# Whole products for the first pairs of layer 2 in a compressed interaction tower

## What is computed

```python
e = jnp.stack([tbl_0[ids[:, 0]], ..., tbl_31[ids[:, 31]]], axis=1)   # 1024 x 32 x 16
x0 = e
xk = x0
for W in (W0, W1, W2):                                             # 32 x 32 x 64, 32 x 64 x 64, 32 x 64 x 64
    xk = jax.nn.relu(jnp.einsum('bmd,bhd,mhk->bkd', x0, xk, W))
    outs.append(jnp.sum(xk, axis=2))
z = jnp.concatenate(outs, axis=1)                                  # 1024 x 192
h = jnp.concatenate([z, dense_ctx], axis=1)                        # 1024 x 208
h = jnp.maximum(h @ W_top1 + b_top1, 0.0)
h = jnp.maximum(h @ W_top2 + b_top2, 0.0)
y = h @ W_top3
```

## Time and profile before

| what | value |
|---|---|
| median of 3 runs | 631.96 us (630.64 to 633.41) |
| the profiled execution | 630.55 us |
| its span in the trace | 628.7 us |
| TensorE busy | 594.6 us, 95% |
| VectorE busy | 585.8 us, 93% |
| GpSimd busy | 443.2 us, 70% |
| ScalarE busy | 355.5 us, 57% |
| mean granted TensorE clock | 0.984 |

### The profile page before, as it was taken

One profiled execution on the slowest core, in us unless ns is written; L12 is line 12 of the kernel. 1 busy time (PEld: TensorE's weight loads), 2 busy tenths in 40 slices (PEclk: granted clock), 3 DMA queues, 4 the chain that ended last, 5 costly groups with the idle time before them and its releaser, 6 DMA issues.

```text
span 628.7 us, 8924 instructions
## 1 busy us (share of the span) xinstructions
PE 594.6 (95%) x3046; PEld 243.0 (39%) x3046; DVE 585.8 (93%) x398; ACT 355.5 (57%) x665; POOL 443.2 (70%) x305
## 2 busy tenths in 40 slices
PE   4398998999999999999999999999999999999988
PEld 4252332234343354334443354334443354334434
DVE  4759999999999989999999999999999999999873
ACT  0173754729394663829385574829385674829361
POOL 5767887888888884988878887988878460806120
PEclk9579999999999999999999999999999999999999
DMA  6899989994997689695999779795999789690000
GB/s 176 192 236 271 210 249 210 274 211 113 252 264 183 137 248 214 205 218 128 238 218 246 154 231 213 230 217 129 221 216 258 155 247 217 212 213 17 2 0 1
DMA packets 60175, 119.82 MB, mean 191 GB/s; under 512 B 15271, under 2 KB 33734, under 8 KB 60054
## 3 DMA queue, kind: packets, MB, share of 16 engines
q1 hardware_dynamic: 49414, 114.69, 73.7%
q0 software_dynamic: 7584, 1.96, 3.8%
q10 hardware_dynamic: 3152, 2.86, 1.7%
HBM read 115.27 MB, written 5.25 MB: 192 GB/s over the span
## 4 chain that ended last, share of the span: by engine, by line
PE 53%; POOL 21%; DVE 12%; issue 7%; ACT 3%; SPq 2%; DMA 1%; DVEq 0%; ACTq 0%; POOLq 0%
PE acc L968 47%; POOL emb L447 12%; POOL z_pool L472 8%; DVE z_dve L529 8%; PE psm L1071 2%; SPq L426 2%; PE psm L1079 2%; DMA x_rot<-in_tbl_dram 1%; DVE z_dve L549 1%; DVE x0b L698 1%; PE acc L983 1%; ACT xq L717 1%; ACT xq L725 1%; ACT xq L771 1%; PE psm L1086 1%
## 5 line engine op out<-in xcount | busy, mean ns | idle before, releaser
L529 DVE TENSOR_TENSOR z_dve<-xq,x0b 128x2048 f32<-128x2048 f32 x179 | 398.5, 2279 | 12.4 <-ACT xq L717 7.5
L968 PE MATMUL acc<-z_dve,w_cin 128*64 128x512 f32 x1688 | 387.2, 597 | 9.9 <-DVE z_dve L529 7.1
L472 POOL TENSOR_TENSOR z_pool<-x0b,xs 128x2048 f32<-128x2048 f32 x45 | 205.3, 4565 | 89.4 <-ACT xs L717 88.9
L447 POOL DMA_INDIRECT emb<-in_tbl_dram,ids_all x224 | 218.3, 974 | 66.3 <-issue 61.3
L968 PEld LDWEIGHTS acc<-z_dve,w_cin 128*64 128x64 f32 x1688 | 127.3, 136 | 230.5 <-issue 166.9
L754 ACT ACTIVATE xq<-acc 64x512 f32<-64x512 f32 x64 | 36.5, 570 | 123.1 <-PE acc L968 122.4
L968 PE MATMUL acc<-z_pool,w_cin 128*64 128x512 f32 x360 | 85.0, 593 | 1.4 <-POOL z_pool L472 1.3
L549 DVE TENSOR_TENSOR z_dve<-xq,x0b 128x1024 f32<-128x1024 f32 x64 | 75.8, 1215 | 6.9 <-ACT xq L754 5.0
L717 ACT ACTIVATE xs<-acc 64x512 f32<-64x512 f32 x124 | 73.4, 592 | 1.7
L771 ACT ACTIVATE xq<-acc 32x512 f32<-32x512 f32 x128 | 72.2, 564 | 1.9
L725 ACT ACTIVATE xq<-acc 32x512 f32<-32x512 f32 x128 | 72.2, 564 | 1.7
(11 more groups left out here) (99 smaller groups left out, 241.8 us busy)
## 6 DMA issues: line engine op xcount, KB each, us to landing
x0b<-x0t SPq DMA_DIRECT2D x120, 512.0 KB, 13.2
x_rot<-x0t SPq DMA_DIRECT2D x60, 512.0 KB
x_rep<-x0t SPq DMA_DIRECT2D x15, 512.0 KB, 7.9
x0b<-x0t SPq DMA_DIRECT2D x16, 256.0 KB, 8.1
emb<-in_tbl_dram,ids_all POOLq DMA_INDIRECT x224
x0t<-emb_t SPq DMA_DIRECT2D x28, 128.0 KB
w_cin<-in_L_rec_W_dram SPq DMA_DIRECT2D x16, 64.0 KB
x_lo<-x0t SPq DMA_DIRECT2D x15, 64.0 KB
```

The source lines that it names most:

```text
L447: nc.gpsimd.indirect_dma_start(out=rows[:, D * f:D * f + D], out_offset=None, in_=tables[f], in_offset=bass.IndirectOffsetOnAxis(ap=ids_al ...
L472: nc.gpsimd.tensor_tensor(z_pool[:, n % ZP_SLOTS, :, :], x0b[b % 2][:, 2 * j:2 * j + 2, :], xs[l - 1][:, :].unsqueeze(1).broadcast_to([P, ...
L529: nc.vector.tensor_tensor(z_dve[:, base % Z_SLOTS, :, :], in0.unsqueeze(1).broadcast_to([P, 2, N]), in1, ALU.mult).then_inc(z_made, 1)
L968: ins = nc.tensor.matmul(acc[l][K * side:K * side + K, :], weights[c], z[:, c, NH * side:NH * side + NH], start=start and c == 0, stop=sto ...
```

## The change

In VectorE's `body`, pair 0 of each order of layer 2 goes through `cin_pair` like the other pairs, in all blocks but the last. `first_pair_of_x2` is called in block 15 alone. Ring slots, counts of `z_made`, and the other engines' programs are as before.

```diff
@@ -603,7 +603,7 @@
                     if k == 1 and not (isinstance(t, int) and t == TILES - 1):
                         fold_sums(t, 0, 1)
                     for i, (v, j) in enumerate(l2_dve(blk(t, k))):
-                        if j == 0:
+                        if j == 0 and is_last(t, k):
                             first_pair_of_x2(t, k, v)
                         else:
                             cin_pair(2, t, k, v, j, 3 + v)
```

## The result

The changed kernel takes 641.98 us (median of 6 runs, 640.65 to 642.36). Against the kernel before on the same chips the ratio is 1.0158, 95% interval 1.0136 to 1.0181: slower by some 10 us. The kernel before was run six times beside it; two of these runs took 1038.6 and 1038.8 us, and the ratio is that to the other four. The forecast was 642.0, in a range of 637 to 645.5.

The account below looks back on a forecast made before the run. No single engine bounds the kernel but a loop of dependences through TensorE, ScalarE and VectorE. Six periods of 72.52 us from 156.86 give +10.55 on 630.55, 641.1 (642.5 by the median); 642.0 taken, range 637 to 645.5.

Parts of the forecast that it names:

- The loop: One tile period's closed path, TensorE, ScalarE's x2-spreading gate, VectorE, TensorE, gate, VectorE: 72.52 us a tile where it was 70.64.
- Its terms: One period's pieces in order: 18.01, 9.41, 20.99, 5.76, 9.42, 8.93 us; each swapped gate including a 0.03 us lag.
- The swapped gate: Layer 2: swapped pair starts 9.41 us after ScalarE's x2 spreading starts, whatever the natural products, ending at 8.96, do.
- TensorE's backlog: TensorE's unfinished work from the odd block is spent at the even block's layer 1; VectorE 1.88 us late by (NAT, 2).
- Ahead of the full periods: Blocks 0 to 2: +0.41, then +0.27 us; block 2's TensorE load at 156.86 where it was at 155.99.
- The late GpSimd product: TensorE's 2.21 us wait at 221.05 for a GpSimd product won't move with the rest and is swallowed.
- VectorE's busy total: Over the whole kernel, VectorE's busy total falls by 4.5 us, with 30 second instructions removed.
- VectorE's idle time: VectorE idle some 2.9 us a tile, most ahead of L529 products and released by ScalarE's L754 and L771.
- TensorE's busy total: Over the whole kernel, TensorE's busy total stays unchanged.
- Rival B: Smaller loss, TensorE's backlog hides all of the odd block: 71.29 us a tile, +3.2, 633.7 us; chance 0.07.
- Rival C: Added TensorE gaps lower its granted clock, 2.4 to 1.2 GHz, for a pair a tile: about +12 more, 654; chance 0.03.
- Rival A: Not slower: VectorE bounds, its queue gets shorter, all four gates past when it arrives: 628.5 or 626.0 us; chance 0.07.

Follow-up runs that it names:

- The longer: Changed kernel plus one 32x512 ACTIVATE ahead of the second side of x2_swp, all blocks but the last: ratio 1.0245 to the kernel before, period 73.69 us.
- the shorter gate: Changed kernel, and separately the kernel before, with three quarters of GpSimd's x2 copy left out in blocks 1 to 15: ratios 1.0081 and 0.9945.
- the wait outside the loop: Kernel before with ScalarE's copy of the sums (zsum_out) put behind x1_swp, no longer ahead of it in even blocks: ratio 1.0000, period 70.65 us.
- the odd-block kernel: Changed kernel with both first pairs whole in odd blocks only, even blocks halved again: 639.45 us, ratio 1.0104 to the kernel before.

## Why the prediction was right, and where it was not

- **The loop** (TensorE to layer 1's end, ScalarE's gate, VectorE, TensorE, gate, VectorE): predicted 72.52 us a tile, measured 72.49. The longer and the shorter gate, and the wait outside the loop, each moved the period as it says. This point is shown.
- **Its terms** were less exact than their sum, and that the sum came out to within 0.03 us is in part luck. Each swapped gate lagged 0.19 us and not 0.03 (+0.32 a tile; I had put 0.13 at the edge of the range). TensorE's two stretches were 17.85 and 5.55 where I had 18.01 and 5.76, -0.37. Before, TensorE came to these two pairs with only some 0.2 us of waiting; now it waits 0.7 there. Why a pair behind a longer wait ends sooner, I only infer: less of the work before is still in its pipeline.
- **The total**: 642.0 against 641.98 is closer than the working. From the profiled execution it gave 641.1, and the profiled execution of the changed kernel took 641.96; the rest was my choice between that and 642.5.
- **The swapped gate binds, the natural one doesn't**: shown by the kernel that halves the natural pair alone.
- **TensorE's backlog is spent** by the even block's layer 1: predicted waits of about 0.5 at its first two pairs, measured 0.59 and 0.86. The first of the new waits comes earlier than I had it, 0.31 over the usual spacing at 338.10, at (SWP, 2) of the odd block's layer 2.
- **Ahead of the full periods** I had +0.87. The load in block 2 stands at 158.35 against 155.99: +2.36. Of this 0.58 is a later start of the first product (47.03, before 46.45) and 0.64 a wait for x0b's DMA at 52.07 (two products of 2.20 after 47.03 would end at 51.43; the bracket leaves out the end of the product ahead). Both come before the first instruction that the change touches:

```profile
47.03 4.49 DVE L529 TENSOR_TENSOR z_dve<-xq,x0b 128x2048 f32<-128x2048 f32 x2 [7.54 <-ACT xq L717]
52.07 8.88 DVE L529 TENSOR_TENSOR z_dve<-xq,x0b 128x2048 f32<-128x2048 f32 x4 [0.55 <-DMA x0b<-x0t]
```

  The other 1.14 are the change, 0.27 more than I had: 0.16 is the lag of block 2's gate, 0.06 that of block 0's (0.09 there). By block 14 the load stands at 592.99 against 581.43, +11.56, so 10.34 without those 1.22; I had 10.55.
- **The late GpSimd product** is swallowed as said: TensorE waits 0.39 over the usual spacing for it, where it was 1.93, and that tile's period is 72.49 like the others:

```profile
223.24 0.20 PEld L968 LDWEIGHTS acc<-z_pool,w_cin 128*64 128x64 f32 x4 [0.67 <-POOL z_pool L472]
```

- **VectorE's busy total** was to fall by 4.5 us; it rose from 585.8 to 586.1, and a tile's from 69.81 to 69.84. That step was wrong. I had warned of durations in the sum and used them for this sign. The busy time counts overlapping instructions once, so the saving was only the 0.07 us a pair of the start-to-start figure, 0.28 a tile. Against it stand two things. Each wait bares the last 0.08 us (2.28 - 2.20) of the instruction ahead of it, and a tile has two waits more, 0.16. And the 0.09 us at layer 1 lie under the end of the product ahead and count as busy. That gives back 0.25 of the 0.28; the 0.06 that are still missing to the measured +0.03 may be the rounding of the rows.
- **VectorE's idle time** was to be 2.9 us a tile and is 2.57 by the brackets. This is the same step seen from the other side: the period less the busy time is 72.49 - 69.84 = 2.65, and the 0.28 that the busy time was to lose would have been idle.
- **TensorE's busy total** was to stay and rose from 594.6 to 600.3 us with unchanged work. The same baring of ends behind its new waits would do this; that it is the cause is inferred.
- **Rival B** (TensorE's backlog hides the odd block, 71.29 a tile) is out by the period and by the odd-block kernel.
- **Rival C** (the clock): the granted clock stays 1.00 through the new waits. Its mechanism exists at a longer wait. In the trace of the kernel with the later sums TensorE stood idle 3.43 us up to 119.99, and the granted clock from 120 to 124 was 0.50, the lower of the two levels:

```profile
120.00:124.00 4.00, 4.00 (x10) 1.36 (x12) 4.00 (x2) 3.89 (x8) 2.96 (x1) 0.50 0.99 375
```

- **Rival A** (the queue gets shorter): its saving is real, 0.07 us a pair, but its condition isn't met, as VectorE waits at all four gates. The swapped pair's half buys 1.06 us behind a gate for that 0.07.

## What to carry to other kernels

Splitting an instruction in two is worth its price where its input comes in pieces and the last piece is late: what counts is how much work is left when the last piece lands (1.14 or 2.20 us here), not how early the first starts. When several engines are above 90% busy, find the closed loop through them and add up its terms. Taking away a wait outside it gains nothing (0.48 us moved elsewhere here). Time added in it shows one for one (2 x 0.60 us), and time taken out of it shows until another term binds (0.85 of 3.6 us a tile). Where two gates lie in a row, the earlier one can hold the engine longest and cost nothing.

## What the runs showed of the hardware

An instruction starts a little behind the end of the one that releases it, and how much depends on the waits ahead of it. In the tiles of the hardware loop a full product behind ScalarE's L771 started 0.19 us behind its end with the ring wait queued last and 0.10 with it queued first, a second half 0.03. Outside the loop, in block 12, it was 0.08 and 0.13, the other way round. So the order of the waits matters by 0.05 to 0.09 us, and which order is better has to be measured where the code stands.

An instruction of VectorE saved between others in a full queue is worth 0.07 us here (2.27 against 2.20), not the 0.15 that the durations give.
